# Down products of keys and values with the weights stationary, and latent rows split straight from PSUM

## The chip, the cores and the metric

One core of one Trainium2 chip. The metric is the device time of one execution in microseconds (us); each number given for the kernel is the median of several executions.

## What is computed

Eight sequences of 256 tokens (2048 rows of width 512) run through four blocks, each added to its input: a block-sparse linear layer, a routed bias (softmax over 64 experts, the best 8), an attention with latent keys and values, and a gated feed-forward. What the change touches is the beginning of the attention:

```python
kc = (hidden_states @ Wk_down.T).reshape(b, s, HK, L).transpose(0, 2, 1, 3)
vc = (hidden_states @ Wv_down.T).reshape(b, s, HK, L).transpose(0, 2, 1, 3)
lat = jnp.concatenate([kc, vc], axis=-1).reshape(b, s, HK * 2 * L)
k_cmp, v_cmp = jnp.split(lat, 2, axis=-1)
k = (k_cmp @ Wk_up.T).reshape(b, s, HK, D).transpose(0, 2, 1, 3)
v = (v_cmp @ Wv_up.T).reshape(b, s, HK, D).transpose(0, 2, 1, 3)
```

with HK = 8 heads, L = 32, D = 128, s = 256. The reshape in the third line mixes tokens and features: row 32 h + m of `lat` holds, for head h, the eight tokens 8 m to 8 m + 7 with their 32 key and 32 value latents each. So feature 64 j + (0 to 63) of a latent row comes from token 8 m + j.

## The kernel before, in words

All products on the matrix engine are made in three passes of fp32r operands, a high part and the rest (`PASSES`): high by high, low by high, high by low. ACT makes a high part (`hi_part`, a copy into fp32r), DVE or POOL the low part (`lo_part`, source less high part).

`first_stages` writes out one program for each engine. The work goes by steps s = 0 to 27 (`head_steps`). In step s the sparse linear layer (`SparseLinear`, 16 tiles of 128 tokens) works on tiles near s, and the routed bias (`RoutedBias`, 7 stages deep) on tiles near i = s - 5; its last stage turns the normed tile into `h3`, columns of tokens, high and low part. Step 18 is i = 13; the last product of the linear layer is in step 18. In each step PE, ACT and DVE first do the bodies of these two, then the key and value tasks assigned to the step; once the steps are over the other tasks follow without them. The order of the tasks is that of `kv_tasks`, the same on every engine, and each engine waits for its semaphores in this order. Tasks are made for each quad (half of the tokens, 1024 rows), and every task has a PSUM bank: `n % 4` in the steps, where banks 4 to 7 belong to the routed bias (and banks 0 to 3 to the linear layer up to step 19), then all eight in turn.

- A **Z** task (line 1280) makes the down product of 128 tokens, those at distance 8 from each other, times all 512 columns of key and value weights: 4 chunks of K by 3 passes, 12 matmuls of 512 columns. The tokens are the stationary operand, read from `h3` at a step of 8 elements (32 bytes). ACT copies the bank to `z`, which lies in the room of `w_raw` (line 1198).
- A **C** task (line 1284) turns 4 blocks of 128x128 of `z` with the unit matrix; the result holds latent features on partitions and latent rows along the columns. ACT and DVE make the two parts of `latent` from it (lines 69 and 74).
- A **K** task (line 1290) and a **V** task (line 1299) make the up products, 6 matmuls of 512 columns each. ACT copies the bank to a stage tile (line 1213), SP stores it to HBM.

There are 8 Z, 8 C, 16 K and 16 V tasks for each quad. In the steps, `head_steps` places 18 tasks of quad 0, from step 20 on (i = 15, once all 8 tiles of the quad are in `h3`). The weights for these products are loaded in 24 pieces (`kv_raw`), each split into parts by ACT and POOL: pieces 0 to 15 in steps 4 to 19, pieces 16 to 23 after step 27, each behind a K task on ACT.

DVE and ACT also make the token operands T1 to T4 of a later product (`TokenOperands`), 16 steps hung on tasks by the lists `sums`, `step_lo_at` and `step_stored`: DVE sums 2 or 3 times 128x512 (lines 358 to 369), ACT the high part, DVE the low part; the next sum waits for the low part before it. Steps 0 to 7 are stored to HBM by SP, three in their place between V stores and five after the last V store of quad 0, behind the store of three blocks of `h3`. Steps 8 to 15 belong to the K and V tasks of quad 1.

The attention then starts with line 1852 (`ps_q`).

## Time and profile before

| | us |
|---|---|
| median of 3 runs (lowest, highest) | 1645.33 (1645.15, 1645.78) |
| the profiled execution, its own time | 1645.85 |
| its span, first to last instruction | 1644.0 |
| PE busy (matmul) | 1615.2, 98% |
| DVE busy | 1163.2, 71% |
| ACT busy | 936.2, 57% |
| POOL busy | 830.8, 51% |
| last V matmul of the first stages ends, attention starts | 259.05 |

The span lacks 1.85 us of the execution's time, at its two ends. Busy times of PE are of overlapping instructions whose ends are modelled, so 98% doesn't say that PE runs at its peak; how far apart the starts of matmuls lie does. "PEld" is the load of a stationary operand, which runs beside the matmul before it.

### The profile page before, as it was taken

The numbers are of one execution on the slowest core, as the hardware profiler recorded it, in microseconds if no ns is written. First come the engines' busy times: TensorE is split into PE (matmuls) and PEld (weight loads), VectorE is DVE, ScalarE is ACT, GpSimd is POOL, SyncE is SP. The second block draws the span as 40 slices with busy tenths as digits, with TensorE's granted clock in tenths as the row PEclk, the third lists the DMA queues.
The fourth block names the chain that finished last, engine by engine and source line by source line (L and its number), as shares of the span: only waits on it lengthen the run. The fifth ranks groups of instructions, "written<-read, shape, count | busy, mean of one in ns | idle before, by whom it ended". The sixth has DMA issues, their size and how long they took to land.

```text
span 1644.0 us, 26456 instructions
## 1 busy us (share of the span) xinstructions
PE 1615.2 (98%) x8298; PEld 1368.8 (83%) x8298; DVE 1163.2 (71%) x2988; ACT 936.2 (57%) x2480; POOL 830.8 (51%) x1243
## 2 busy tenths in 40 slices
PE   7999999999999999999999999999999999999999
PEld 5778887888888888888888888888888788878887
DVE  7963365776776776777677767767767688787676
ACT  5865455665665765765666566657657443434432
POOL 6852004544634634644545445446446397709752
PEclk9999999999999999999999999999999999999999
DMA  5002753111111111134111111111111121102211
GB/s 187 24 18 83 282 197 123 39 65 39 52 65 39 52 64 39 44 100 183 47 52 39 65 40 52 65 39 52 65 40 26 41 70 64 39 32 91 64 65 52
DMA packets 62490, 114.99 MB, mean 70 GB/s; under 512 B 5584, under 2 KB 25040, under 8 KB 58256
## 3 DMA queue, kind: packets, MB, share of 16 engines
q1 hardware_dynamic: 62352, 113.30, 20.8%
q8 instruction: 68, 1.11, 0.3%
q14 instruction: 70, 0.57, 0.1%
HBM read 84.97 MB, written 28.31 MB: 69 GB/s over the span
## 4 chain that ended last, share of the span: by engine, by line
PE 90%; DVE 5%; issue 2%; ACT 1%; POOL 1%; DMA 1%; DVEq 0%; SPq 0%; POOLq 0%; ACTq 0%
PE ps_q L1912 21%; PE ps_q L1852 19%; PE f_ps_r L2393 11%; PE ps_o L1894 8%; PE f_ps_y L2412 7%; PE ps_s L1870 5%; PE ps_s L1882 5%; PE ps_s L1868 3%; PE kv_banks L1280 3%; PE kv_banks L1290 3%; PE kv_banks L1299 3%; PE f_ps_r L2377 1%; DVE bn_ln L97 1%; DVE h_lo L74 1%; DVE x L744 0%
## 5 line engine op out<-in xcount | busy, mean ns | idle before, releaser
L1912 PE MATMUL ps_q<-kv_w_hi,o_hi 128*128 128x512 f32 x512 | 202.2, 395 | 0.0
L1912 PE MATMUL ps_q<-kv_w_lo,o_hi 128*128 128x512 f32 x512 | 199.7, 390 | 0.0
L1912 PE MATMUL ps_q<-kv_w_hi,o_lo 128*128 128x512 f32 x512 | 199.6, 390 | 0.0
L74 POOL TENSOR_TENSOR kv_w_lo<-w_raw,kv_w_hi 128x512 fp32r<-128x512 f32 x128 | 163.2, 1294 | 56.3 <-ACT kv_w_hi L69 56.2
L1852 PE MATMUL ps_q<-h_hi,kv_w_hi 128*128 128x512 f32 x448 | 180.1, 402 | 0.1
L1852 PE MATMUL ps_q<-h_lo,kv_w_hi 128*128 128x512 f32 x448 | 175.1, 391 | 0.0
L1852 PE MATMUL ps_q<-h_hi,kv_w_lo 128*128 128x512 f32 x448 | 175.0, 391 | 0.0
L1681 DVE TENSOR_TENSOR x<-ps_q,x 128x512 f32<-128x512 f32 x128 | 88.1, 688 | 96.4 <-PE ps_q L1912 96.4
L69 ACT ACTIVATE kv_w_hi<-w_raw 128x512 fp32r<-128x512 f32 (+1 forms) x240 | 126.7, 567 | 45.5 <-POOL w_raw L300 42.0
L1495 ACT ACTIVATE prob<-prob,neg_max 128x128 f32<-128x128 f32 x256 | 100.4, 392 | 89.3 <-DVE neg_max L1651 89.3
L1440 POOL TENSOR_SCALAR prob<-prob,inv_sum 128x128 f32<-128x128 f32 x256 | 95.4, 373 | 109.5 <-DVE inv_sum L1656 109.4
L69 ACT ACTIVATE o_hi<-ps_o 128x512 fp32r<-128x512 f32 x128 | 76.3, 596 | 126.3 <-PE ps_o L1894 126.2
L74 POOL TENSOR_TENSOR h_lo<-v_raw,h_hi 128x512 fp32r<-128x512 f32 x32 | 41.3, 1291 | 184.8 <-ACT h_hi L69 184.8
L74 DVE TENSOR_TENSOR o_lo<-ps_o,o_hi 128x512 fp32r<-128x512 f32 x128 | 88.3, 690 | 56.2 <-ACT o_hi L69 56.1
L1497 ACT ACTIVATE prob<-prob,neg_max 128x256 f32<-128x256 f32 x256 | 127.0, 496 | 0.0
L1441 POOL TENSOR_SCALAR prob<-prob,inv_sum 128x256 f32<-128x256 f32 x256 | 122.8, 480 | 0.0
L1912 PEld LDWEIGHTS ps_q<-kv_w_lo,o_hi 128*128 128x128 f32 x512 | 96.1, 188 | 20.3
L1912 PEld LDWEIGHTS ps_q<-kv_w_hi,o_lo 128*128 128x128 f32 x512 | 96.3, 188 | 18.6
L1912 PEld LDWEIGHTS ps_q<-kv_w_hi,o_hi 128*128 128x128 f32 x512 | 96.2, 188 | 18.6
L295 POOL TENSOR_TENSOR w_raw<-w_raw 128x512 f32<-128x512 f32 x16 | 20.7, 1297 | 178.9 <-DVE kv_w_lo L74 178.9
L2393 PE MATMUL f_ps_r<-h_hi,kv_w_hi 128*128 128x512 f32 x280 | 109.1, 390 | 0.5 <-issue 0.4
L1882 PEld LDWEIGHTS ps_s<-ident,prob 128*128 128x128 f32 x768 | 91.2, 140 | 21.6 <-DVE prob_t_lo L74 3.9
(236 smaller groups left out, 4844.3 us busy)
## 6 DMA issues: line engine op xcount, KB each, us to landing
w_raw<-in_wq_g SPq DMA_DIRECT2D x16, 1024.0 KB, 4.8
w_raw<-in_wo_g SPq DMA_DIRECT2D x16, 1024.0 KB, 4.7
k_raw<-k_scratch SPq DMA_DIRECT2D x32, 256.0 KB, 3.4
v_raw<-v_scratch SPq DMA_DIRECT2D x32, 256.0 KB, 3.8
f_gate_raw<-in_gate_c SPq DMA_DIRECT2D x10, 512.0 KB, 4.9
f_up_raw<-in_up_c SPq DMA_DIRECT2D x10, 512.0 KB, 3.6
f_down_raw<-in_down_c SPq DMA_DIRECT2D x10, 512.0 KB, 4.1
x<-in_x SPq DMA_DIRECT2D x16, 256.0 KB, 2.8
```

Source lines behind the costliest of these rows:

```text
L69: return act.activation(parts[HI], src, ACT.Copy)
L74: return dve.tensor_tensor(parts[LO], src, parts[HI].bitcast(F32), ALU.subtract)
L1440: pool.tensor_scalar(prob[:, b, h, 0:P], prob[:, b, h, 0:P], inv_sum[:, b, h, 0:1], 1.0, ALU.mult, ALU.mult)
L1441: pool.tensor_scalar(prob[:, b, h, P:3 * P], prob[:, b, h, P:3 * P], inv_sum[:, b, h, 1:2], 1.0, ALU.mult, ALU.mult).then_inc(normed, 1)
L1495: act.activation(prob[:, b, h, 0:P], prob[:, b, h, 0:P], ACT.Exp, scale=-1.0, bias=neg_max[:, b, h, 0:1], accum_out=row_sum[:, b, h, 0:1])
L1497: act.activation(prob[:, b, h, P:3 * P], prob[:, b, h, P:3 * P], ACT.Exp, scale=-1.0, bias=neg_max[:, b, h, 1:2], accum_out=row_sum[:, b, ...
L1852: done = pe.matmul(ps_q[:, i, :], left[s][:, c, i * HEAD:(i + 1) * HEAD], right[t][:, c, :], start=(c == 0 and m == 0), stop=(c == 1 and m ...
L1882: done = pe.transpose(ps_t[:, (b + blk) % 2, h * P:(h + 1) * P], prob[:, b, h, blk * P:(blk + 1) * P], ident[:, :])
L1894: done = pe.matmul(ps_o[:, half, :], v[i][:, 2 * b + tile, :], prob_t[j][blk], start=(n == 0 and m == 0), stop=(n == len(blocks) - 1 and m ...
L1912: done = pe.matmul(ps_q[:, half, :], o[b][i][:, half, h, :], wo[j][:, h, :], start=(h == 0 and m == 0), stop=(h == GROUP - 1 and m == 2))
L2393: last = pe.matmul(bank(kind, k, name), stationary[a], feed.operand(right)[b][:, c, :], start=(c == 0 and m == 0), stop=(c == 1 and m == 2))
L2412: last = pe.matmul(ps_y[:, t % 4, :], inner[m, n][a][:, t % 4 * P:(t % 4 + 1) * P], down[m][b], start=(m == 0 and i == 0), stop=(m == chun ...
```

## The change

The Z task now takes 128 columns of the weights as its stationary operand and 512 tokens in a row (a pair of sequences) as the moving one. Its result has 128 down features (two heads, each with 32 key and 32 value latents, since the weights are packed by head) on partitions and tokens along the columns. That is already the orientation of `latent`, so z and the C tasks go away: ACT and DVE take the bank in four pieces each, one for each head of the two (`one`, a half of the source's partitions) and for odd and even tokens (`odd`, the half of the partitions that it goes to). A piece is 64 partitions by 4x2x32 = 256 elements, read from PSUM at a step of 8 elements. There are 4 Z tasks for each pair of sequences, 8 for each quad, still 12 matmuls of 512 columns each.

Tasks start in step 18 (i = 13), two in every step, 20 in all: 8 Z, 8 K of pair 0, 4 K of pair 1. All 24 pieces of weights are split in steps 4 to 27. Operand steps are hung on other tasks, and five instead of three are stored in their place between the V stores.

```diff
 def kv_tasks():
     for quad in range(2):
-        down = [("Z", quad, j, 0) for j in range(8)]
-        flip = [("C", quad, jp, hg) for jp in range(4) for hg in range(2)]
...
-        tasks += down[0:4] + flip[0:2] + down[4:6] + flip[2:4] + down[6:8] + flip[4:6]
-        tasks += (keys[0:2] + flip[6:8] if quad else flip[6:8] + keys[0:2]) + keys[2:] + values
+        tasks += [("Z", quad, pair, heads) for pair in range(2) for heads in range(KV_HEADS // 2)]
+        tasks += [("K", quad, pair, g) for pair in range(2) for g in range(KV_HEADS)]
+        tasks += [("V", quad, tile, part) for tile in range(8) for part in range(2)]
 def head_steps():
-    ready = TILES // 2 + RoutedBias.DEPTH
-    group = (2, 2, 3, 2, 2, 2, 3) + (2,) * (RoutedBias.STEPS - ready - 7)
+    ready = TILES + 2 - FIRST_ROUTED
...
-        count = group[i - ready] if i >= ready else 0
+        count = 2 if i >= ready else 0
 def first_stages(...):
             if not before:
                 if bank_of[n] >= 4:
                     eng.wait_ge(routed.lo_done, TILES)
+                elif bank_of[n] >= 2:
+                    eng.wait_ge(linear.x_done, TILES)
                 else:
                     eng.wait_ge(linear.lo_done, TILES)
-                    eng.wait_ge(linear.x_done, TILES)
...
+        def outlets(n):
+            _, _, pair, heads = tasks[n]
+            for one in range(2):
+                src = bank[one * HALF:(one + 1) * HALF, bank_of[n], :].rearrange("p (b m c o) -> p c b m o", b=2, c=4, o=2)
+                for odd in range(2):
+                    yield ([p[odd * HALF:(odd + 1) * HALF, :, 2 * pair:2 * pair + 2, 2 * heads + one, :] for p in latent], src[:, :, :, :, odd])
...
-        sums = [("V", 0, 0, 0), ("V", 0, 2, 0), ("V", 0, 4, 0), ("V", 0, 6, 0), ("Z", 1, 1, 0), ("Z", 1, 3, 0), ("Z", 1, 5, 0), ("Z", 1, 7, 0),
+        sums = [("V", 0, 0, 0), ("V", 0, 1, 1), ("V", 0, 2, 1), ("V", 0, 4, 0), ("V", 0, 5, 1), ("V", 0, 6, 1), ("Z", 1, 0, 2), ("Z", 1, 1, 2),
                 ("K", 1, 0, 4), ("K", 1, 0, 6), ("K", 1, 1, 0), ("K", 1, 1, 2), ("K", 1, 1, 4), ("K", 1, 1, 6), ("V", 1, 0, 0), ("V", 1, 2, 0)]
-        step_lo_at.update({at["C", 1, 2, 1]: 7, at["V", 1, 4, 0]: 15})
-        step_stored = {at[task]: j for j, task in enumerate((("V", 0, 2, 1), ("V", 0, 4, 1), ("V", 0, 6, 1)))}
+        step_lo_at.update({at["K", 1, 0, 1]: 7, at["V", 1, 4, 0]: 15})
+        step_stored = {at[task]: j for j, task in enumerate((("V", 0, 2, 0), ("V", 0, 3, 0), ("V", 0, 4, 1), ("V", 0, 6, 0), ("V", 0, 7, 0)))}
 # act_program, task(n)
                 if kind == "Z":
-                    act.activation(z[:, a // 2 % 2, :, a % 2, :].rearrange("p h (t l) -> p h t l", t=2),
-                                   bank[:, bank_of[n], :].rearrange("p (t h l) -> p h t l", t=2, h=KV_HEADS), ACT.Copy).then_inc(z_done, 1)
+                    for parts, src in outlets(n):
+                        hi_part(act, parts, src).then_inc(hi_done, 1)
 # dve_program, task(n)
-                if n in lo_count:
-                    dve.wait_ge(hi_done, lo_count[n])
-                    parts, src = outlet(n)
-                    lo_part(dve, parts, src).then_inc(lo_done, 1)
+                if n in parts_done:
+                    dve.wait_ge(linear.xb_done, TILES)
+                    for m, (parts, src) in enumerate(outlets(n)):
+                        dve.wait_ge(hi_done, parts_done[n] + m // 2 * 2 + 2)
+                        lo_part(dve, parts, src).then_inc(lo_done, 1)
 # pe_program, task(n)
                 if kind == "Z":
-                    pe.wait_ge(routed.lo_done, (quad + 1) * TILES // 2)
+                    pe.wait_ge(routed.lo_done, 4 * (2 * quad + a) + 4)
                     for c in range(KC):
                         for m, (u, v) in enumerate(PASSES):
-                            tokens = h3[u][:, c, quad * SPAN:(quad + 1) * SPAN].rearrange("p (n j) -> p n j", j=8)[:, :, a]
-                            last = pe.matmul(out, tokens, down_w[v][:, c, :], start=(c == 0 and m == 0), stop=(c == KC - 1 and m == 2))
-                elif kind == "C":
-                    pe.wait_ge(z_done, down_count[at[("Z", quad, 2 * a + 1, 0)]])
-                    for h in range(4):
-                        last = pe.transpose(out[:, h * P:(h + 1) * P], z[:, a % 2, 4 * b + h, :, :].rearrange("p j l -> p (j l)"), ident[:, :])
+                            last = pe.matmul(out, down_w[u][:, c, b * P:(b + 1) * P], h3[v][:, c, (2 * quad + a) * PAIR:(2 * quad + a + 1) * PAIR],
+                                             start=(c == 0 and m == 0), stop=(c == KC - 1 and m == 2))
                 elif kind == "K":
-                    if (a, b) == (0, 0):
-                        pe.wait_ge(lo_done, lo_count[at[("C", quad, 1, 1)]])
+                    if b == 0:
+                        latent_made(pe, quad, a)
```

The program of PE, steps 18 to 20, before: behind the last matmul of the linear layer (787) come three bodies of the routed bias (988 to 1018), and then the first matmul of a Z task (1280).

```order
255 L787 MATMUL kv_banks<-w_lo,h_hi 128x512
256 L988 MATMUL kv_banks<-ident,r_chosen 128x128
257 L996 MATMUL kv_banks<-ident,h 128x128 x4
...
260 L1018 MATMUL kv_banks<-ident,h 128x128 x4
261 L988 MATMUL kv_banks<-ident,r_chosen 128x128
...
265 L1018 MATMUL kv_banks<-ident,h 128x128 x4
266 L988 MATMUL kv_banks<-ident,r_chosen 128x128
...
270 L1018 MATMUL kv_banks<-ident,h 128x128 x4
271 L1280 MATMUL kv_banks<-kv_w_hi,h_hi 128x512
```

The same place of PE after the change (Z is line 1266 there).

```order
255 L786 MATMUL kv_banks<-w_lo,h_hi 128x512
256 L987 MATMUL kv_banks<-ident,r_chosen 128x128
257 L995 MATMUL kv_banks<-ident,h 128x128 x4
...
260 L1017 MATMUL kv_banks<-ident,h 128x128 x4
261 L1266 MATMUL kv_banks<-h_hi,kv_w_hi 128x512
...
284 L1266 MATMUL kv_banks<-h_lo,kv_w_hi 128x512
285 L987 MATMUL kv_banks<-ident,r_chosen 128x128
...
289 L1017 MATMUL kv_banks<-ident,h 128x128 x4
290 L1266 MATMUL kv_banks<-h_hi,kv_w_hi 128x512
```

Two Z tasks (24 matmuls) now stand behind the body of step 18 and of step 19 each, where bodies followed each other with nothing between them.

The program of ACT after the change, from the end of step 18 to the first half of step 19 (line 68 is `hi_part`).

```order
119 L933 ACTIVATE h1t<-kv_banks 128x512
120 L68 ACTIVATE kv_w_hi<-kv_raw 128x256
121 L68 ACTIVATE latent_hi<-kv_banks 64x4x2x32 x8
122 L903 ACTIVATE r_exp,r_total<-logits,r_neg_max 128x64
123 L908 ACTIVATE x<-x,r_combined 128x512
```

Before, the body of step 19 (904) followed at once on `kv_w_hi`; the eight pieces of 64 partitions now stand between them, and they wait for the Z tasks of their step.

## Rows read from the trace of the kernel before

**Rows 1.** The page: the span, the granted clock by 40th parts, and part 4, the chain by engine.

```profile
span 1644.0 us, 26456 instructions
...
PEclk9999999999999999999999999999999999999999
...
PE 90%; DVE 5%; issue 2%; ACT 1%; POOL 1%; DMA 1%; DVEq 0%; SPq 0%; POOLq 0%; ACTq 0%
```

**Rows 2.** The chain that ended last, in order of time: start us, us, what.

```profile
106.13 6.03 PE kv_banks L1280 x24
...
138.01 2.95 PE kv_banks L1280 x12
...
144.75 21.78 PE kv_banks L1290 x96
...
188.29 11.73 PE kv_banks L1280 x48
200.03 0.87 PE kv_banks L1284 x8
...
237.29 21.76 PE kv_banks L1299 x96
259.05 13.88 PE ps_q L1852 x60
...
274.99 6.19 DMA w_raw<-in_wo_g
```

**Rows 3.** Groups by form, 0 to 330 us: busy us, mean ns | idle us before them.

```profile
L1280 PEld LDWEIGHTS kv_banks<-kv_w_hi,h_lo 128*128 128x128 f32 x64 | 21.2, 331 | 0.2
...
L1290 PEld LDWEIGHTS kv_banks<-latent_hi,kv_w_lo 128*128 128x128 f32 x64 | 12.0, 188 | 2.4
...
L74 DVE TENSOR_TENSOR latent_lo<-kv_banks,latent_hi 128x512 fp32r<-128x512 f32 x16 | 10.3, 682 | 15.0 <-ACT latent_hi L69 15.0
...
L69 ACT ACTIVATE latent_hi<-kv_banks 128x512 fp32r<-128x512 f32 x16 | 8.8, 600 | 0.0
...
L914 ACT ACTIVATE r_chosen_t<-kv_banks 128x128 f32<-128x128 f32 x16 | 4.1, 258 | 0.2 <-PE kv_banks L988 0.2
...
L962 DVE TENSOR_TENSOR logits<-kv_banks,r_bias 128x64 f32<-128x64 f32 x16 | 3.4, 212 | 0.7 <-PE kv_banks L1010 0.7
```

**Rows 4.** Timeline of PE: start us, us, what [idle before <-releaser].

```profile
96.03 0.61 PE L1018 MATMUL kv_banks<-ident,h 128*128 128x128 f32 x4
97.97 0.30 PE L988 MATMUL kv_banks<-ident,r_chosen 128*128 128x128 f32 x1 [1.33 <-ACT h1t L934]
...
105.88 0.61 PE L1280 MATMUL kv_banks<-kv_w_hi,h_hi 128*128 128x512 f32 x1
...
112.00 0.27 PE L988 MATMUL kv_banks<-ident,r_chosen 128*128 128x128 f32 x1
...
114.60 0.61 PE L1280 MATMUL kv_banks<-kv_w_hi,h_hi 128*128 128x512 f32 x1
...
144.12 0.63 PE L996 MATMUL kv_banks<-ident,h 128*128 128x128 f32 x4 [0.99 <-DVE h_lo L74]
```

**Rows 5.** Timeline of ACT, the first and last instruction of step 18.

```profile
93.88 0.35 ACT L904 ACTIVATE r_exp<-logits,r_neg_max 128x64 f32<-128x64 f32 x1 [1.34 <-DVE r_neg_max L974]
...
97.72 0.41 ACT L69 ACTIVATE kv_w_hi<-kv_raw 128x256 fp32r<-128x256 f32 x1
```

**Rows 6.** Timeline of DVE, the first and last instruction of step 19.

```profile
98.59 0.66 DVE L744 TENSOR_TENSOR x<-kv_banks,x 128x512 f32<-128x512 f32 x1
...
103.25 0.17 DVE L101 BATCH_NORM_AGGREGATE mv_ln<-bn_ln 128x2 f32<-128x6 f32 x1
```

**Rows 7.** Timeline of ACT, the high parts of operand steps 8, 14 and 15.

```profile
223.42 0.62 ACT L69 ACTIVATE h_hi<-op_sum 128x512 fp32r<-128x512 f32 x1
...
241.94 0.63 ACT L69 ACTIVATE h_hi<-op_sum 128x512 fp32r<-128x512 f32 x1 [1.24 <-DVE op_sum L364]
...
251.47 0.63 ACT L69 ACTIVATE h_hi<-e_bias 128x512 fp32r<-128x512 f32 x1 [5.91 <-DVE e_bias L358]
```

More of the change, by code:

```diff
@@ L1026, in kv_tasks @@
     for quad in range(2):
-        down = [("Z", quad, j, 0) for j in range(8)]
-        flip = [("C", quad, jp, hg) for jp in range(4) for hg in range(2)]
-        keys = [("K", quad, pair, g) for pair in range(2) for g in range(KV_HEADS)]
-        values = [("V", quad, tile, part) for tile in range(8) for part in range(2)]
-        tasks += down[0:4] + flip[0:2] + down[4:6] + flip[2:4] + down[6:8] + flip[4:6]
-        tasks += (keys[0:2] + flip[6:8] if quad else flip[6:8] + keys[0:2]) + keys[2:] + values
+        tasks += [("Z", quad, pair, heads) for pair in range(2) for heads in range(KV_HEADS // 2)]
+        tasks += [("K", quad, pair, g) for pair in range(2) for g in range(KV_HEADS)]
+        tasks += [("V", quad, tile, part) for tile in range(8) for part in range(2)]
     return tasks
 def head_steps():
-    ready = TILES // 2 + RoutedBias.DEPTH
-    group = (2, 2, 3, 2, 2, 2, 3) + (2,) * (RoutedBias.STEPS - ready - 7)
+    ready = TILES + 2 - FIRST_ROUTED
     steps, n = [], 0
@@ L1056, in first_stages @@
     at = {task: n for n, task in enumerate(tasks)}
-    hi_order = [n for n, task in enumerate(tasks) if task[0] == "C"]
-    lo_count = {n: k + 1 for k, n in enumerate(hi_order)}
     down_order = [n for n, task in enumerate(tasks) if task[0] == "Z"]
-    down_count = {n: k + 1 for k, n in enumerate(down_order)}
+    parts_done = {n: 4 * k for k, n in enumerate(down_order)}
     stage_order = [n for n, task in enumerate(tasks) if task[0] in "KV"]
@@ L1068, in first_stages @@
         pieces_of = {"Z": KV_DOWN // KV_PIECE, "K": (KV_DOWN + KV_UP) // KV_PIECE, "V": KV_PIECES}
-        z = query.raw[:, :, :].rearrange("p (j h) (h2 t l) -> p j (h h2) t l", j=2, h2=4, t=2)
         bank = ps("kv_banks", [P, 8, HID], st)
@@ L1150, in pool_program, with store @@
                 routed.pool_body(pool, i)
-                if 0 <= p < HEAD_PIECES:
+                if 0 <= p < KV_PIECES:
                     piece_lo_part(pool, p)
-            for p in range(HEAD_PIECES, KV_PIECES):
-                piece_lo_part(pool, p)
             query.make(pool, 0)
+        def store(sp, n):
+            kind, quad, a, b = tasks[n]
+            if kind == "Z":
+                return
+            k = stage_count[n]
+            sp.wait_ge(staged, k + 1)
+            if k >= STAGES:
+                sp.wait_ge(stored[k % STAGES], 16 * (k // STAGES))
+            if kind == "K":
+                pair = 2 * quad + a
+                dst = k_scr[b, :, pair * PAIR:(pair + 1) * PAIR]
+            else:
+                pair = 2 * quad + a // 4
+                dst = v_scr[pair, :, a % 4, b * HID:(b + 1) * HID]
+            sp.dma_start(dst, stage_tile(k)).then_inc(stored[k % STAGES], 16)
+            if n in step_stored:
+                operands.store_step(sp, step_stored[n])
+            if n == at[("V", 0, 7, 1)]:
+                sp.wait_ge(routed.lo_done, TILES)
+                operands.store_blocks(sp)
+                for j in range(len(step_stored), 8):
+                    operands.store_step(sp, j)
+            if n == at[("K", 1, 0, 3)]:
+                query.load(sp, wq_g, 0)
@@ L1187, in act_program @@
+            for _, _, p, now in steps:
+                if 0 <= p < KV_PIECES - 2:
+                    load_piece(sp, p + 2)
+                for n in now:
+                    store(sp, n)
+            for n in range(paired, len(tasks)):
+                store(sp, n)
         def act_program(act):
@@ L1191, in task @@
                 if kind == "Z":
[L1192 to L1213 removed]
+                    for parts, src in outlets(n):
+                        hi_part(act, parts, src).then_inc(hi_done, 1)
+                else:
+                    k = stage_count[n]
+                    if k >= STAGES:
+                        act.wait_ge(stored[k % STAGES], 16 * (k // STAGES))
+                    if STAGED <= k < STAGED + STAGES:
+                        act.wait_ge(routed.lo_done, TILES)
+                    act.activation(stage_tile(k), bank[:, bank_of[n], :], ACT.Copy).then_inc(staged, 1)
                     if n in given_at:
@@ L1227, in act_program @@
                 routed.act_body(act, i)
-                if 0 <= p < HEAD_PIECES:
+                if 0 <= p < KV_PIECES:
                     piece_hi_part(act, p)
@@ L1293, in task @@
                 else:
-                    if (a, b) == (0, 0):
-                        pe.wait_ge(lo_done, lo_count[at[("C", quad, 3, 1)]])
+                    if a % 4 == 0 and b == 0:
+                        latent_made(pe, quad, a // 4)
                     for c in range(2):
```

68 lines of the change are left out of this document (9 added, 59 removed).

## The prediction, made before the change was run

> **What bounds the kernel now.** I read the page first. PE makes 90% of the chain that ended last, and its clock is the full one in all 40 slices, so the level of 2.4 GHz is not in question here; the span of 1644.0 us is PE's program plus its waits [rows 1]. Then I read that chain in order of time, which shows the places touched: Z tasks among the steps from 106.13 us, K tasks from 144.75, Z and C tasks of quad 1 from 188.29, the last V tasks until the attention starts at 259.05 [rows 2]. From 106 us on the chain lies on PE nearly all the time, so every microsecond that PE saves or idles there less is one off the whole. Third, the groups by form, for what a Z matmul waits for and what copies on ACT and DVE cost [rows 3]. Fourth, the timeline of PE: between 96 and 106 us, steps 18 to 20, PE waits for ACT and DVE behind each body, because no task is there yet [rows 4]; and those of ACT and DVE, for how full their steps are [rows 5, 6].
>
> **The change part by part.**
>
> *1. Turns go.* 64 turns leave PE. Eight take 0.87 us on the chain [rows 2], so 8 x 0.87 = **7.0 us**.
>
> *2. Z matmuls at another pace.* In quad 1, 48 matmuls take 11.73 us, 0.244 each; in quad 0, 24 take 6.03 and twelve 2.95, that is 0.251 and 0.246; I take 0.247 for the mean of all 192. K and V matmuls with the same 512 columns take 21.78 / 96 = 0.227 [rows 2]. The row of loads says why: a stationary operand read from tokens at a step of 8 elements takes 331 ns with 0.2 us of idle time in 64, one in a row takes 188 ns and leaves room [rows 3]. The new Z task loads weights in a row and moves tokens in a row, as K does, so I give it K's pace: 192 x 0.020 = **3.9 us**. I take this to be sure within 0.3.
>
> *3. Idle time before the first task.* The last four turns of step 18's body start at 96.03 [rows 4] and take half of the 0.87 us of eight [rows 2], so it ends at 96.47, and Z starts at 105.88. Between them lie two bodies, each 2.60 us when nothing is waited for (112.00 to 114.60) [rows 4]. 9.41 - 5.20 = **4.2 us** of idle, into which tasks now move: two Z behind the body of step 18 and two behind step 19's. PE does the same work, earlier.
>
> *4. The last wait of the steps.* Before, PE waited 0.99 us at 144.12, because short C tasks stood in the last steps [rows 4]; now two K tasks (2.7 us) stand in each of them. **1.0 us**.
>
> Together 16.1 us less. Against it:
>
> *5. Pieces on ACT and DVE.* A bank was copied to z and then split from a second bank; now it is split once, in four pieces of 256 elements on 64 partitions. No row shows such a piece. From 128 to 512 columns an ACT copy from PSUM goes from 258 to 600 ns [rows 3], so 256 lie at 258 + 342 / 3 = 0.37 us; on DVE 64 columns take 212 ns and 512 take 682 [rows 3], 1.05 ns for each more, so 256 lie at 0.41 us, of which 0.14 is fixed. That is my value, whole durations without overlap, since a piece changes its partitions from one to the next. The bound below is the same with the overlap seen between two instructions in a row, about 0.1 us less. The bound above: the only row that reads fp32 at a step of 8 elements is the weight load, 331 against 188 ns, a factor of 1.76; then a DVE piece is 0.14 + 0.27 x 1.76 = 0.62, and at the very most as long as 512 in a row, 0.68 [rows 3].
>
> Is that hidden? In the four steps with Z tasks (18 to 21) PE needs 2.6 + 24 x 0.227 + 0.1 for starting behind turns = 8.15 us. ACT needs its body, 93.88 to 98.13, 4.25 us [rows 5], and 8 x 0.37 = 3.0: 7.2 us. DVE needs 98.59 to 103.42, 4.83 us, with the linear layer's last sum in it [rows 6], and 8 x 0.41 = 3.3: 8.1 us. All three fit, DVE barely, and only in steps 18 and 19, since the linear layer's part is missing in 20 and 21. The covers are there because PE waits in each body for what the others did one step earlier. One wait is in the way: in step 19 the third Z task uses bank 2, free after the linear layer's last sum (DVE 744), which stands behind the pieces of step 18. Those end about 2.4 us after the second Z; then the sum, 0.7; PE comes after a body of 2.6. I take **0.4 us**.
>
> *6. Shorter steps 22 to 27.* Two K tasks are 2.7 us, a body 0.4 to 2.3, so a step is 3.2 to 5 us, while in each the low part of a tile must be ready for PE's next turn: a stage copy (0.5), ACT's body up to the high part (about 2.6 of the 4.25 [rows 5]), the split (0.6 and 0.7) come to about 4.3 us, where PE needs 4.1 in step 23. **0.3 us**. The pieces of weights now taken in these steps (0.41 us on ACT [rows 5], the rest on POOL) fit.
>
> *7. Quad 1.* ACT needs 4 x 0.37 = 1.5 and DVE 1.6 us for each Z of 2.72 us: fit. K waits for pieces of its own pair of sequences, with four Z or eight K tasks in between: 10.9 us ahead. SP issues the stores of operand steps 5 to 7 in front of the first K store, as it did with 3 to 7; but the low part of step 7 now comes behind the last Z, and the K stores, and so the stage tiles of ACT, wait for it: I reckon that ACT makes the high part of step 8 1.2 to 2.5 us later against the V tasks. From there the operand steps are paced by themselves: from step 8 at 223.42 to step 14 at 241.94, 3.1 us for each against 2.7 for two tasks of PE [rows 7], so the delay stays until step 15. At step 15 ACT stands until 251.47 [rows 7]; its next copy ends at 252.6, and PE, with 8 banks, would need it at 237.29 + 13 x 1.36 = 254.97 [rows 2]. Of these 2.4 us little or nothing is left. **0.3 us**.
>
> SP's own queue: piece loads now lie between K stores in other steps, two steps ahead of their use; the wait for the query weights moves by one K task, and they are needed 11 tasks later. No cost. POOL gets nothing but the last pieces of weights earlier. What follows 259.05 starts from the same work in the same order, so it moves as a whole.
>
> **Sum:** 7.0 + 3.9 + 4.2 + 1.0 - 0.4 - 0.3 - 0.3 = 15.1. The profiled execution took 1645.85 us (span 1644.0 and 1.85 around it); 1645.85 - 15.1 = 1630.75, and the median of the runs, 1645.33, lies 0.52 below the profiled one: **1630.2 us**.
>
> **The rivals.**
>
> *A. Pieces read slowly.* If a piece costs what the bound above says, DVE needs 4.8 + 8 x 0.62 = 9.8 us in a step where PE needs 8.15, ACT about 8.5. That is 1.6 us lost in each of up to four steps, less where the linear part is missing: 2 to 6 us, so 1632 to 1636. For it: 32 bytes between elements did slow the one row that has them. Against: that row is PE reading SBUF, this is ACT and DVE reading PSUM. The Trainium skill, SBUF — State Buffer, section "Door 1: The DMA port swizzle", speaks for it: PSUM has lines of 8 bytes, and each access that crosses to a new line pays; in a piece every element does. No row here shows it for ACT or DVE, and the page has no price; by the rule the time would be this rival's, about 1634.
>
> *B. Operand steps stop PE in quad 1.* If the delay in 7 is 4 us instead of 2, PE stands at V tasks 13 to 15 for about 2 us, and the attention's first weight parts are late by as much: 1632 to 1634. For it: a margin of 2.4 us; against: eight banks and that ACT catches up afterwards.
>
> *C. Nothing comes of it.* The time saved before 259 us is waited away later, at a wait that hangs on transfers and not on PE. For it: a transfer of 6.19 us lies in the chain at 274.99 [rows 2]; against: it fetches weights into a room that PE's own products and their sums must first give free, so it moves with them. 1643 to 1648.
>
> *D. Slower.* The pieces are the bound. Over the 64 pieces on DVE the loss is 32 d - 13.6 in the four steps (4 x (8 d + 4.8 - 8.2)) and 32 d - 27 in quad 1 (32 pieces and 5.6 us of operand steps against 21.8 us of Z and 10.9 of K tasks). It eats 15.1 us at d = 0.87 us, over twice my value; at d = 1.2 us the loss is 36, and the time 1645.3 - 15.1 + 36 = 1666. Nothing in the profile has 256 elements that slow.
>
> That the change doesn't do what it says can hardly be: tokens as moving operand and weights as stationary ones in a row stand in the program.
>
> **How the numbers follow.** My forecast (1628 to 1632) 0.62; A 0.16; B 0.12; C 0.05; D 0.03; 0.02 for less than 1628. With the costs of 5 to 7 at nothing the time is 1645.33 - 16.1 = 1629.2, and the gains may be mis-sized by 1 us, so the range starts at 1628.0; it reaches to 1635.5, most of A and all of B. 0.2% of the time is 3.3 us, about what can be told from no change. Faster by more than that: 0.92; within it, C in the main: 0.05; slower: 0.03.
>
> **What would show it.** Right if: Z matmuls are 0.227 us apart and their loads 190 ns; no turns of z; PE starts Z at about 96.4 and idles under 1 us in the steps; the attention starts at 243 to 245 us; pieces of 0.35 to 0.45 us. Wrong if: DVE or ACT pieces show 0.6 us or more and PE's idle time ahead of 987 or 995 is released by them (A); PE waits at V tasks of quad 1 for copies (B); the start of the attention moves by 15 us and the end by less (C).

## The result, and the profile after

The changed kernel takes **1637.45 us** (median of 5 runs, 1636.5 to 1638.69) against 1645.78 us (5 runs, 1645.15 to 1646.75) of the kernel before in the same session; the ratio is 0.9945, with a 95% interval of 0.9934 to 0.9957. The gain is 8.3 us where 15.1 were forecast, and the time lies 1.95 us above the end of the range (1635.5). The profiled execution took 1638.69 us with a span of 1636.8: 7.2 us less than the profiled one of before, and this is the sum that the rows below have to explain. It was the slowest of the five; its mean granted clock is 0.998, that of the next three 0.999, that of the fastest 1.000.

The page of the changed kernel, as in [rows 1]: 64 matmuls fewer, and a clock that the slices of 41 us still show as full.

```profile
span 1636.8 us, 26389 instructions
...
PE 1607.9 (98%) x8234; PEld 1352.8 (83%) x8234; DVE 1179.7 (72%) x3036; ACT 942.5 (58%) x2512; POOL 830.4 (51%) x1243
...
PEclk9999999999999999999999999999999999999999
```

The chain that ended last, in order of time (start and duration in us, engine, what), as in [rows 2]. L1266 is now Z, L1273 K, L1282 V, L1835 the first products of the attention.

```profile
96.93 5.50 PE kv_banks L1266 x24
106.28 5.49 PE kv_banks L1266 x24
...
152.58 8.18 PE kv_banks L1273 x36
160.76 21.76 PE kv_banks L1282 x96
182.52 21.76 PE kv_banks L1266 x96
204.28 21.76 PE kv_banks L1273 x96
226.04 10.89 PE kv_banks L1282 x48
246.62 5.97 PE kv_banks L1282 x18
252.59 13.87 PE ps_q L1835 x60
```

The 96 Z matmuls of quad 1 take 21.76 us, 0.227 each, as K and V do; before there were 96 matmuls, the first 48 of them 0.244 us apart and the others 0.250, and 32 turns between them. Z starts at 96.69 (the chain counts it from 96.93), forecast 96.4. But the pairs of Z tasks in the steps follow one another at 9.35 us instead of 8.15 (96.93, 106.28, and two more), and quad 0 ends at 182.52, only 5.8 us earlier than the 188.29 of [rows 2]. And of quad 1's V phase, which without a stop is 21.76 us, 26.55 are gone when the attention starts at 252.59: 6.5 us earlier than 259.05. The rest of the program takes 1384.2 us after it, before 1385.0; so 5.8 + 0.7 + 0.7 = 7.2.

By groups of one form (line, engine, operation, busy us, mean ns of one, idle time before), as in [rows 3], from 96 to 226 us: the load of weights in a row, and the pieces.

```profile
L1266 PEld LDWEIGHTS kv_banks<-h_hi,kv_w_lo 128*128 128x128 f32 x64 | 12.0, 188 | 2.4
```

ACT's groups of the changed kernel:

```profile
L68 ACT ACTIVATE latent_hi<-kv_banks 64x256 fp32r<-64x256 f32 x64 | 24.2, 378 | 10.5 <-PE kv_banks L1266 9.2
```

DVE's groups of the changed kernel:

```profile
L73 DVE TENSOR_TENSOR latent_lo<-kv_banks,latent_hi 64x256 fp32r<-64x256 f32 x64 | 27.0, 423 | 17.4 <-ACT latent_hi L68 15.7
```

A piece takes 0.378 us on ACT and 0.423 on DVE, where 0.37 and 0.41 were taken. So the length of the pieces is not what was mis-sized. Where does PE stand, then? First the steps, in PE's timeline (start, duration, operation, and in brackets the idle time before it with who ended it), as in [rows 4]:

```profile
102.25 0.27 PE L987 MATMUL kv_banks<-ident,r_chosen 128*128 128x128 f32 x1
...
103.66 1.00 PE L1009 MATMUL kv_banks<-router,h1t 128*128 128x64 f32 x8
105.65 0.63 PE L1017 MATMUL kv_banks<-ident,h 128*128 128x128 f32 x4 [0.99 <-ACT r_chosen_t L913]
...
136.37 0.63 PE L995 MATMUL kv_banks<-ident,h 128*128 128x128 f32 x4 [0.75 <-DVE h_lo L73]
```

PE waits 0.99 us ahead of the last turns of the body of step 19, and so it does in steps 20 and 21, for `r_chosen_t`, a copy of ACT. Each wait costs 1.2 us of pace (9.35 less 8.15). ACT and DVE at this time, where [rows 5, 6] showed steps without tasks:

```profile
99.72 1.58 ACT L68 ACTIVATE latent_hi<-kv_banks 64x256 fp32r<-64x256 f32 x4 [1.29 <-PE kv_banks L1266]
102.45 1.58 ACT L68 ACTIVATE latent_hi<-kv_banks 64x256 fp32r<-64x256 f32 x4 [1.14 <-PE kv_banks L1266]
104.06 0.35 ACT L903 ACTIVATE r_exp<-logits,r_neg_max 128x64 f32<-128x64 f32 x1
...
104.41 0.80 ACT L908 ACTIVATE x<-x,r_combined 128x512 f32<-128x512 f32 x1
105.23 0.28 ACT L913 ACTIVATE r_chosen_t<-kv_banks 128x128 f32<-128x128 f32 x1
```

DVE's timeline of the changed kernel:

```profile
103.33 1.78 DVE L73 TENSOR_TENSOR latent_lo<-kv_banks,latent_hi 64x256 fp32r<-64x256 f32 x4 [0.95 <-ACT latent_hi L68]
105.14 0.69 DVE L743 TENSOR_TENSOR x<-kv_banks,x 128x512 f32<-128x512 f32 x1
```

The four pieces of the second Z task start at 102.45, when its last matmul is done, and `r_chosen_t` of the *next* body stands behind them. PE's last turns (L1017) go to the bank that this copy empties. It empties it in the same step, not one step behind. In step 19 a second wait lies under this one: its first Z task needs bank 2, which DVE's sum of the linear layer (L743) frees at 105.83, while PE, at a pace of 8.15 us, would have come at 96.69 + 8.15 = 104.84. Steps 20 and 21 have no such sum.

Second, quad 1: DVE, then SP's queue, then ACT, then PE.

```profile
209.52 1.78 DVE L73 TENSOR_TENSOR latent_lo<-kv_banks,latent_hi 64x256 fp32r<-64x256 f32 x4 [1.57 <-ACT latent_hi L68]
211.34 0.69 DVE L73 TENSOR_TENSOR op_out_lo<-e_bias,op_out_hi 128x512 fp32r<-128x512 f32 x1
```

SP's timeline of the changed kernel:

```profile
212.06 0.32 SPq L387 DMA_DIRECT2D operand_scratch<-op_out_hi  x1
212.42 0.43 SPq L387 DMA_DIRECT2D operand_scratch<-op_out_lo  x1
212.95 1.90 SPq L1167 DMA_DIRECT2D k_scratch<-kv_stage  x4
```

SP's timeline of the kernel before, the first K stores of quad 1:

```profile
218.24 2.36 SPq L1173 DMA_DIRECT2D k_scratch<-kv_stage  x3
```

ACT's timeline of the changed kernel:

```profile
215.85 0.60 ACT L1201 ACTIVATE kv_stage<-kv_banks 128x512 f32<-128x512 f32 x1 [3.53 <-DMA k_scratch<-kv_stage]
216.35 0.62 ACT L68 ACTIVATE h_hi<-op_sum 128x512 fp32r<-128x512 f32 x1
...
235.94 0.63 ACT L68 ACTIVATE h_hi<-op_sum 128x512 fp32r<-128x512 f32 x1 [1.24 <-DVE op_sum L363]
...
245.45 0.63 ACT L68 ACTIVATE h_hi<-e_bias 128x512 fp32r<-128x512 f32 x1 [5.89 <-DVE e_bias L357]
```

PE's timeline of the changed kernel:

```profile
246.62 0.71 PE L1282 MATMUL kv_banks<-kv_w_hi,latent_hi 128*128 128x512 f32 x1 [2.90 <-ACT kv_stage L1201]
...
248.83 0.63 PE L1282 MATMUL kv_banks<-kv_w_lo,latent_hi 128*128 128x512 f32 x1
249.26 0.63 PE L1282 MATMUL kv_banks<-kv_w_hi,latent_hi 128*128 128x512 f32 x1
...
250.11 0.42 PE L1282 MATMUL kv_banks<-kv_w_lo,latent_hi 128*128 128x512 f32 x1
```

The low part of operand step 7 (211.34) comes behind the pieces of all Z tasks; SP issues the stores of step 7's high and low part at 212.06 and 212.42, and only then that of the first K tile, 13.1 us ahead of the first V task (226.04); before it was 19.1 us ahead (218.24 and 237.29). ACT had waited 3.53 us for that stage tile. It makes the high part of step 8 at 216.35, 9.7 us ahead of the first V task, where [rows 7] had 223.42, 13.9 us ahead. The shift of 4.2 us is still there at step 14 (235.94, 9.9 us behind the start of V; before 241.94, 4.7 us behind it: 5.2). At step 15 ACT stands until 245.45, all eight banks are full, and PE stops for 2.90 us. The wait of ACT itself is no part of the change: it is 5.89 us where the kernel before had 5.91. In both, DVE first makes two low parts of query weights, and two of the three sums of step 15 then take 1.66 us each, where those of the other steps take 0.69. Behind the stop the matmuls are 0.427 us apart until 250.1, and a window of the trace (us, then busy time of each engine, granted clock, DMA share and GB/s) gives the clock:

```profile
245.00:250.00 5.00, 3.38 (x8) 2.71 (x9) 1.71 (x3) 4.38 (x9) 1.63 (x1) 0.67 0.50 193
```

0.67 in the mean of these 5 us, in which PE first idled and then ran at 1.2 GHz; from 250.1 on it is 2.4. The eight matmuls at the low level take 3.49 us instead of 1.82, another 1.7 us. A second such stretch lies at 275 to 280 us (clock 0.75), with a wait of 1.64 us for DVE in it. Neither comes in every execution: the fastest of the five, at 1636.5 us, has a mean clock of 1.000. The Trainium skill, TensorE: Matmul & The Clock Gate, section "Back-to-back issue gap", gives N / 1.2 ns between isolated matmuls of N columns at the low level and N / 2.4 + 2.5 at the high one, which for 512 columns makes an estimate of 427 and 216 ns. The trace agrees with the first (0.427 us) and shows 0.227 us for the second.

So two places hold what is missing: about 3.6 us in the steps (call it loss 1) and 4.6 in quad 1 (2.9 + 1.7, loss 2). Both readings are of a trace, and each has a rival: loss 1 may come from pieces that are too long rather than from where they stand, loss 2 from the extra work of ACT and DVE rather than from the place of step 7.

### The profile page after: what moved, and what is told of

The parts are those of the page before. It is cut to its first block, busy times and chain, and to the rows that moved or that the text cites. A ratio compares the mean times of both kernels' runs of the same rounds, so it can differ in the third digit from the quotient of the medians.

```text
span 1636.8 us, 26389 instructions
## 1 busy us (share of the span) xinstructions
PE 1607.9 (98%) x8234; PEld 1352.8 (83%) x8234; DVE 1179.7 (72%) x3036; ACT 942.5 (58%) x2512; POOL 830.4 (51%) x1243
## 4 chain that ended last, share of the span: by engine, by line
PE 93%; DVE 2%; ACT 2%; POOL 1%; issue 1%; DMA 1%; SPq 0%; DVEq 0%; ACTq 0%; POOLq 0%
PE ps_q L1895 21%; PE ps_q L1835 19%; PE f_ps_r L2376 11%; PE ps_o L1877 8%; PE f_ps_y L2395 7%; PE ps_s L1853 5%; PE ps_s L1865 5%; PE ps_s L1851 3%; PE kv_banks L1266 3%; PE kv_banks L1273 3%; PE kv_banks L1282 2%; PE kv_banks L786 2%; PE f_ps_r L2360 1%; PE kv_banks L1002 1%; PE kv_banks L1009 0%
## 5 line engine op out<-in xcount | busy, mean ns | idle before, releaser
L1835 PE MATMUL ps_q<-h_hi,kv_w_hi 128*128 128x512 f32 x448 | 180.7, 403 | 0.1
L1835 PE MATMUL ps_q<-h_lo,kv_w_hi 128*128 128x512 f32 x448 | 175.5, 392 | 0.0
L1835 PE MATMUL ps_q<-h_hi,kv_w_lo 128*128 128x512 f32 x448 | 175.2, 391 | 0.0
L2376 PE MATMUL f_ps_r<-h_hi,kv_w_lo 128*128 128x512 f32 x280 | 108.9, 389 | 0.0
```

The lines of the kernel that those rows point to most:

```text
L1835: done = pe.matmul(ps_q[:, i, :], left[s][:, c, i * HEAD:(i + 1) * HEAD], right[t][:, c, :], start=(c == 0 and m == 0), stop=(c == 1 and m ...
L2376: last = pe.matmul(bank(kind, k, name), stationary[a], feed.operand(right)[b][:, c, :], start=(c == 0 and m == 0), stop=(c == 1 and m == 2))
```

## The experiments

All kernels are edits of the changed kernel; "span" and places in it are of their profiled execution. The ratio is to the kernel before, run on the same chip in the same session. Its median went from 1645.78 to 1647.27 us from session to session, so medians of two sessions compare to about 1.5 us; the places in the traces are the sharper measure.

### e_late: pieces and copies one step later

```diff
+            held = ()
             for s, i, p, now in steps:
...
-                for n in now:
+                for n in held:
                     task(n)
-            for n in range(paired, len(tasks)):
+                held = now
+            for n in list(held) + list(range(paired, len(tasks))):
                 task(n)
```

The same in ACT's and in DVE's program; PE's order stays.

> The changed kernel, but in steps 18 to 27 ACT and DVE do the tasks of a step only after the body of the next step. Theory 1 (my own now): in steps 19 to 21 PE's last turns wait, within the same step, for ACT's copy of the chosen weights (0.99 us each, three times, and 9.35 us from one step's first Z to the next instead of 8.15), because that copy stands behind eight pieces which wait for the Z tasks. Expected: these waits gone, 8.15 to 8.3 us for a step, the last V task of quad 0 ends 4 to 4.5 us earlier (182.5 to about 178), the whole 1633 to 1634 us. Theory 2: the pieces themselves are the load (ACT 7.4, DVE 8.4 us a step); then the order makes no difference and a step stays over 9 us. The V tasks of quad 1 keep their wait of 2.9 us by both.

Measured: 1634.55 us (1633.93 to 1635.1), ratio 0.9931 (0.9916 to 0.9946). The chain, and the groups of PE from 96 to 253 us that have idle time:

```profile
97.06 5.47 PE kv_banks L1270 x24
105.22 5.47 PE kv_banks L1270 x24
...
179.62 21.76 PE kv_banks L1270 x96
```

PE's groups of e_late:

```profile
L1286 PE MATMUL kv_banks<-kv_w_hi,latent_hi 128*128 128x512 f32 x64 | 25.6, 400 | 2.7 <-ACT kv_stage L1201 2.7
...
L995 PE MATMUL kv_banks<-ident,h 128*128 128x128 f32 x36 | 5.4, 274 | 1.3 <-DVE h_lo L73 1.3
```

The pairs are 8.16 us apart, what the prediction worked out for PE alone; the waits for `r_chosen_t` are gone, with pieces of the same length. In their place 1.3 us stand at L995 in step 23 (0.75 in the changed kernel). Quad 0 ends 2.9 us earlier, at 179.62, where about 178 was expected. Loss 1 is the order: the bodies of ACT and DVE stand behind the pieces. In steps 20 and 21 this is the copy alone; in step 19 the edit also puts the linear layer's sum ahead of the pieces, at 99.02, and the run doesn't part the two. The stop in the V phase stays at 2.7 us.

### e_flat and e_stay: are the pieces slow?

e_flat reads 256 neighbouring elements for each piece instead of elements at a step of 8, so that a latent row gets other tokens:

```diff
-yield ([p[odd * HALF:(odd + 1) * HALF, ...] for p in latent], src[:, :, :, :, odd])
+flat = bank[one * HALF:(one + 1) * HALF, bank_of[n], 256 * odd:256 * odd + 256].rearrange("p (c b m) -> p c b m", c=4, b=2)
+yield ([p[odd * HALF:(odd + 1) * HALF, ...] for p in latent], flat)
```

> The changed kernel, but each piece reads 256 neighbouring elements of its bank instead of every eighth and so on, so that the latents are of other tokens. If elements read at a step of 8 from PSUM are slow, ACT's 378 ns and DVE's 423 ns for a piece fall clearly (below 0.33 and 0.36), and steps 19 to 21 get shorter by over 1 us. If not (my theory), both stay within 10 ns, and the time within 0.5 us.

Measured, one execution: 1636.69 us, span 1634.9. The pieces:

```profile
L68 ACT ACTIVATE latent_hi<-kv_banks 64x256 fp32r<-64x256 f32 x64 | 24.2, 378 | 10.5 <-PE kv_banks L1267 9.2
```

DVE's groups of e_flat:

```profile
L73 DVE TENSOR_TENSOR latent_lo<-kv_banks,latent_hi 64x256 fp32r<-64x256 f32 x64 | 27.0, 423 | 17.4 <-ACT latent_hi L68 15.7
```

378 and 423 ns, the same to the nanosecond, and the pairs stay 9.34 us apart. Reading PSUM at a step of 32 bytes costs ACT and DVE nothing here. The Trainium skill, SBUF — State Buffer, section "Door 1: The DMA port swizzle", gives PSUM lines of 8 bytes and says that an access pattern which isn't contiguous slows matmuls; it gives no rule for ACT and DVE. Rival A had carried the rule over to them, and for these reads of fp32 the measurement doesn't bear that out.

e_stay sends each piece to the half of the partitions that it is read from, so that keys and values of the two heads are mixed up in `latent`:

```diff
-p[odd * HALF:(odd + 1) * HALF, :, 2 * pair:2 * pair + 2, 2 * heads + one, :]
+p[one * HALF:(one + 1) * HALF, :, 2 * pair:2 * pair + 2, 2 * heads + odd, :]
```

> The changed kernel, but each piece goes to the same half of the partitions that it comes from (odd tokens to the other head's place, so the latents are mixed up). In the changed kernel four pieces take 1.58 us on ACT and 1.78 on DVE, each starting when the one before is done (0.40 and 0.45 apart), while copies of 512 columns started 0.1 us before the end of the last. If the change of partitions from piece to piece forbids this overlap, pieces now come 0.30 (ACT) and 0.35 us (DVE) apart, and steps 19 to 21 get shorter by 0.3 us or so each. If it is not that, nothing changes.

Measured, one execution: 1634.46 us, span 1632.7. In the timelines of ACT and DVE:

```profile
99.39 1.32 ACT L68 ACTIVATE latent_hi<-kv_banks 64x256 fp32r<-64x256 f32 x4 [1.28 <-PE kv_banks L1266]
```

DVE's timeline of e_stay:

```profile
100.14 1.55 DVE L73 TENSOR_TENSOR latent_lo<-kv_banks,latent_hi 64x256 fp32r<-64x256 f32 x4 [1.50 <-ACT latent_hi L68]
```

PE's groups of e_stay from 94 to 253 us:

```profile
L1282 PE MATMUL kv_banks<-kv_w_hi,latent_hi 128*128 128x512 f32 x64 | 25.0, 391 | 1.4 <-ACT kv_stage L1201 1.4
```

Four pieces take 1.32 us instead of 1.58 on ACT and 1.55 instead of 1.78 on DVE, though one piece alone is as long as before (372 and 418 ns): where the output stays in the same partitions, an instruction starts while the one in front of it still runs (on ACT 0.32 us apart in the mean instead of 0.40, on DVE 0.38 instead of 0.45; the output changes its half once among the four). The prediction had taken the durations whole for this reason. The Trainium skill, VectorE: DVE Perf Modes, section "Two Vector instructions with no wait between them", holds an instruction whose output starts in another group of partitions than the last output; on DVE the trace agrees, and the price is 0.07 us in this mean. On DVE the SBUF input of a piece (`latent_hi`) changes its half together with the output, so this run doesn't part the two; on ACT only the output changes. That section doesn't speak of ACT.

The pairs come to 9.07 us apart and the waits for `r_chosen_t` to 2.2 us, so the length of the pieces has a part in loss 1, but a small one: 0.3 us a step, of 1.2. In loss 2 its part is larger. With step 7 at its old place, the high part of step 8 comes at 213.28, 11.2 us ahead of V (224.50) instead of 9.7, the stop falls from 2.9 to 1.4 us, and no matmul behind it is slow. The attention starts at 248.55, 4.0 us earlier than in the changed kernel.

### e_store7, e_early: what stops PE in quad 1?

e_store7 moves the two stores of step 7 in SP's queue behind the fourth K store:

```diff
-                for j in range(len(step_stored), 8):
+                for j in range(len(step_stored), 7):
                     operands.store_step(sp, j)
             if n == at[("K", 1, 0, 3)]:
+                operands.store_step(sp, 7)
```

> The changed kernel, but SP stores operand step 7 behind the fourth K store of quad 1 instead of ahead of the first. Theory 1: the high part of step 8 waits for a stage tile, whose store waits in SP's queue for the low part of step 7; then it comes 1.5 to 2 us earlier (6.7 to 6.3 us... that is at about 8 us before the V tasks of quad 1 start less, from 9.7 us to over 11 us ahead of them), PE's wait of 2.9 us at the fourteenth V task shrinks to 1 us or so, and the half clock behind it (3.8 us of granted 1.2 GHz) shrinks or goes: 1634.5 to 1636.5 us. Theory 2: the operand steps are late because of their own sums (DVE), not because of the store: nothing moves, 1637 to 1638.

Measured: 1635.49 us (1635.32 to 1636.06), ratio 0.9937 (0.9923 to 0.9952). The stop, and the clock around it:

```profile
L1283 PE MATMUL kv_banks<-kv_w_hi,latent_hi 128*128 128x512 f32 x64 | 25.0, 391 | 2.1 <-ACT kv_stage L1202 2.1
```

And the window of e_store7, with the clock behind the busy times:

```profile
245.00:250.00 5.00, 4.37 (x18) 3.30 (x18) 1.29 (x2) 4.82 (x10) 2.49 (x2) 1.00 0.78 299
```

The high part of step 8 comes at 213.65, 11.9 us ahead of V (225.52) instead of 9.7, but the stop falls only from 2.9 to 2.1 us: from step 8 to step 14 (234.59) it now takes 20.9 us, where the changed kernel took 19.6 and the kernel before 18.5. No matmul behind the stop is slow, but this can't be put down to the edit: in e_flat, with a stop of 2.83 us at the same place, none is slow either (0.23 us apart from 245.87 on). Half a confirmation: the first K tile comes sooner, and at step 8 what ends last is now DVE's sum, still behind the last pieces. Later ACT waits 3.67 us for a K store (until 221.28, ahead of step 10), where the changed kernel waited 2.09. I take this for the price of the two stores that now stand in front of the later K stores; no run shows it alone.

e_early takes up both at their root, the sums of steps 6 and 7:

```diff
-("V", 0, 6, 1), ("Z", 1, 0, 2), ("Z", 1, 1, 2),
+("V", 0, 6, 1), ("Z", 1, 0, 0), ("Z", 1, 0, 3),
...
-step_lo_at.update({at["K", 1, 0, 1]: 7, at["V", 1, 4, 0]: 15})
+step_lo_at.update({at["Z", 1, 1, 0]: 7, at["V", 1, 4, 0]: 15})
```

> The changed kernel, but operand steps 6 and 7 hang on the first and fourth Z task of quad 1 (not on the third and seventh), and the low part of step 7 on the fifth Z task (not on the second K task). Theory 1: PE's wait of 2.9 us in the V tasks of quad 1 comes from step 7's low part standing behind the pieces of all eight Z tasks; from it SP's queue, the K stores, and the high part of step 8 (9.7 us ahead of the V tasks, 13.9 before the change) are late, and all later steps. Now the high part of step 8 comes about 3 us earlier, over 12.5 us ahead of the V tasks; PE's wait in the V tasks goes, and with it the half clock behind it; 1632.5 to 1634 us. Theory 2: the operand steps are held by their transfers (ACT waited 2.4 to 3.0 us for stores in each of steps 2 to 5): then they come no earlier, and the time stays above 1636.

Measured: 1633.87 us (1633.64 to 1634.29), ratio 0.9922 (0.9907 to 0.9937). ACT's timeline, and what is left of PE's idle time there:

```profile
213.88 0.63 ACT L68 ACTIVATE h_hi<-op_sum 128x512 fp32r<-128x512 f32 x1 [0.86 <-DVE op_sum L357]
...
242.00 0.63 ACT L68 ACTIVATE h_hi<-e_bias 128x512 fp32r<-128x512 f32 x1 [5.91 <-DVE e_bias L357]
```

PE's groups of e_early:

```profile
L1835 PE MATMUL ps_q<-h_hi,kv_w_hi 128*128 128x512 f32 x7 | 2.8, 403 | 0.5 <-issue 0.5
```

The high part of step 8 is at 213.88, 12.0 us ahead of V (225.92), that of step 15 at 242.00; no V task waits, and no matmul of the phase is slow. The attention starts at 248.19, 4.4 us earlier than in the changed kernel, and the span is 4.7 us shorter, with the same work on every engine. So the place of steps 6 and 7 is enough to bring or remove loss 2. It is not the only thing that counts: e_stay, with shorter work at the old place, took away half of the stop. The delay of step 8 is made of both, what stands in front of it and how long that takes.

### e_start20: what was the early start worth?

`ready` two steps later, so Z starts in step 20 and 16 tasks lie in the steps:

```diff
-    ready = TILES + 2 - FIRST_ROUTED
+    ready = TILES + 4 - FIRST_ROUTED
```

> The changed kernel, but tasks start in step 20 as they did before, 16 of them in the steps. If the early start gives what I forecast less what the in-step waits take (4.2 against 2 x 1.2), the last V of quad 0 ends 1.5 to 2 us later than in the changed kernel, and the whole takes 1639 to 1640. If starting early is worth its full 4.2 us, it is 1641 to 1642; if it is worth nothing, 1637 to 1638.

Measured: 1640.77 us (1640.01 to 1641.4), ratio 0.9967 (0.9955 to 0.998): 3.3 us more than the changed kernel, between the two ranges that were expected. That is what the early start is worth here, its 4.2 us less what it brings, to about 1 us: by the ratios it is 3.6, and the attention starts 2.7 us later (255.33). Two bodies wait 1.3 us each for ACT's `h1t` (2.7 us at L987), one instead of three waits at L1017 (1.0 us), and behind the wait of 1.35 us at 102.38 the turns and products are slow (granted clock 0.76 from 100 to 106 us):

```profile
102.38 0.30 PE L987 MATMUL kv_banks<-ident,r_chosen 128*128 128x128 f32 x1 [1.35 <-ACT h1t L933]
...
103.77 1.92 PE L1002 MATMUL kv_banks<-e_bias,r_chosen_t 128*128 128x512 f32 x2
```

Two matmuls of 512 columns take 1.92 us where the changed kernel's take 1.02. In the kernel before they took 1.02 at the same place behind the same wait (1.34 us), so such a wait need not bring the slow turns.

### e_both, e_all, e_mix: both repairs together

e_both has the edits of e_late and e_early, e_all that of e_store7 as well.

> Both edits: tasks in the steps done by ACT and DVE after the next step's body, and operand steps 6 and 7 earlier. If the two losses are apart from each other, they add: 2.9 us (e_late against the changed kernel) and what e_early gives; 1629.5 to 1631.5 us, which is my forecast for the change itself.

> As the one with both edits, and step 7 stored behind the fourth K store as well. If the V tasks' wait is gone already, nothing more comes of it: within 0.5 us of the other. If some wait is left, up to 1 us less.

Measured: e_both **1631.05 us** (1630.4 to 1631.15), ratio 0.9904 (0.9887 to 0.992); e_all 1632.03 (1631.85 to 1632.66), ratio 0.9911 (0.9897 to 0.9926). The chain of e_both:

```profile
179.69 21.76 PE kv_banks L1270 x96
...
223.21 21.76 PE kv_banks L1286 x96
```

The V phase of quad 1 takes its 21.76 us, and the attention starts at 245.29, 1.3 us behind what the prediction's terms give (259.05 - 15.1 = 243.95). The waits left are 1.3 us at L995 and 0.3 ahead of the attention, where those terms hold 1.0 us of losses, and Z starts 0.5 us later than forecast (96.88); 0.2 us are not assigned. Together the repairs bring the start of the attention 7.3 us forward, alone 3.1 (249.53) and 4.4: they add up. In e_all the third repair costs 1.0 us, where at most 0.5 was expected: the stores of step 7 now stand in front of later K tiles, and a stop of 1.1 us is back in the V phase.

e_mix lags only the tasks of Z by a step and leaves K and V copies in their own:

```diff
-                for n in held:
+                for n in list(held) + [n for n in now if tasks[n][0] != "Z"]:
                     task(n)
-                held = now
+                held = [n for n in now if tasks[n][0] == "Z"]
```

> Lags only the splits of Z tasks by one step on ACT and DVE (copies of K and V tasks are done in their own step again), with the operand sums 6 and 7 at the earlier tasks. Theory: the wait of 1.3 us at the turns of h (995) in step 23 comes from the chain of a step, in which lagged copies stand; with copies of K tasks in their own step as in the changed kernel it falls to about 0.75 us (what the changed kernel showed there), the waits at 1017 stay away, and the attention starts 0.5 us earlier, at about 244.8; time 1630.5. Rival: in step 22 the lagged pieces and the step's own copies stand together on ACT, four tasks in one step, and the wait is as long or longer (1.3 to 2.5 us): 1631 to 1632.

Measured: 1630.69 us (1630.55 to 1630.76), ratio 0.9904 (0.9887 to 0.992). The wait at L995 is 1.28 us at 136.84, the same as in e_both, so the theory of this run fell: the wait doesn't depend on where the K copies of step 22 stand. The span is 0.5 us shorter, but its Z tasks start at 96.25 where e_both's start at 97.13, and the attention at 244.63 against 245.29: this difference of 0.9 us lies ahead of the first instruction that the edit moves, so these runs don't make one faster than the other. What sets the wait in step 23 stays open beyond its releaser, DVE's `h_lo`.

## Why the prediction was wrong

The sign held, and the gains were sized well. The time was wrong because two covers were taken as given which the trace of before could not show, and which the new order took away.

- **1, turns (7.0 us), and 2, pace of Z (3.9).** Right. Of quad 1, e_early shows 65.8 us from the end of quad 0 to the attention, the changed order of work without a stop; before it was 70.8. The difference of 5.0 is half of 10.9 less the 0.5 us at L1835.
- **3, idle time before the first task (4.2).** The early start was right: Z at 96.7 against 96.4, within the scatter of this place (96.0 in e_mix to 96.9 in e_both, ahead of anything that those edits move). e_start20 finds it worth 3.3 us net of the waits that it brings.
- **5, pieces.** Their size was nearly right: 0.378 and 0.423 us for 0.37 and 0.41, but on DVE they start 0.45 us apart, so eight take 3.6 us and not 3.3. With a body of 4.83 us this makes 8.4 us, over the 8.15 of PE, in the step with the linear layer's sum. That was not what cost the time: in e_late the same work goes at 8.16. The step that failed is the sentence "The covers are there because PE waits in each body for what the others did one step earlier." The copy `r_chosen_t` is awaited in the same step. ACT had to do the pieces of a Z task that had just ended (102.45), 1.2 us of its body, and then this copy, while PE had products only until 104.66. **0.4 us were forecast; 3 x 1.2 = 3.6 came.** The forecast 0.4 us were for bank 2 in step 19. That wait was mis-sized too: the bank came free 1.0 us behind PE's time, hidden under the wait for the copy. Adding up busy time tells whether the work fits, not whether it is in time. The program of ACT printed before the prediction already had the eight pieces in front of the whole body.
- **4 and 6.** The wait of 0.99 us at 144.12 is gone. At L995 the changed kernel waits 0.75 us, forecast 0.3.
- **7, quad 1.** The right mechanism with the wrong sizes. The step that failed is "I reckon that ACT makes the high part of step 8 1.2 to 2.5 us later against the V tasks": it was 4.2, and 5.2 at step 14, against the margin of 2.4 us, which was right (5.2 - 2.4 = 2.8, and PE stood 2.9). The prediction had the chain in full (low part behind the last Z, K stores behind it, stage tiles behind them) but shows no working for its size; the first K store came 6.0 us later against the V tasks, the high part 4.2. Nor did the delay stay as it was: steps 8 to 14 took 19.6 us instead of 18.5, with ACT waiting for K stores ahead of steps 9 and 10. And the price of the stop left out the clock: 1.7 us for eight matmuls at 1.2 GHz, in those executions that have them. **0.3 us were forecast; 4.6 came.**

The two excesses, 3.2 and 4.3, with 0.4 in 6 and 0.3 for the start, make 8.2 us; 0.7 us gained behind the start of the attention goes the other way. 15.1 - 8.2 + 0.7 = 7.6, against 7.2 in the profiled executions; 0.4 us is not assigned. That the medians differ by 8.3 fits the clocks: 3.5 us at 1.2 GHz lower the mean of 1637 us by 0.001, and the profiled execution, at 0.998, had both slow stretches where the median one had room for one.

Of the rivals, **B** (0.12) was the mechanism of quad 1, with 2.9 us of stop at the fourteenth V task for its "about 2 us", and it came on top of loss 1, which no rival had. **A** is refuted by e_flat: its symptom, PE's idle time in the bodies released by ACT and DVE, did appear, but the step of 8 elements had no part in it. **C** did not happen: from e_both to the changed kernel 7.3 us at the start of the attention are 7.4 us of the span. **D** was far off. The range ended at 1635.5 because each case was taken alone; with B's 2 to 4 us and 3 of a wait in the steps together it would have ended at 1637.2, still 0.25 us short of the time. With both places repaired the change comes to about what was forecast for it: 1631.05 and 1630.69 against 1630.2. There is some luck in this, since the waits left in e_both are not those of terms 5 and 7.

## What to carry to other kernels

When work is moved beside other work, don't stop at the sum of busy times for a step: take each wait of the engine that sets the pace, ask whether what it waits for is made in the same step or one earlier, and count what now stands in front of it on its engine. Follow a queue to its end: a low part that is late held up a store, that a stage tile, that a copy 34 us later (211.34 to 245.45). An engine's copies of what was just computed belong behind its part of the next body, if banks allow it, and a stop of PE of some 3 us should be priced with and without matmuls at half clock behind it: both came here.

## What the runs showed of the hardware

- ACT and DVE read fp32 from PSUM at a step of 32 bytes as fast as in a row (378 and 378 ns, 423 and 423, for 64x256), while PE's weight load from SBUF at that step takes 331 ns instead of 188 [rows 3].
- For these pieces, on both engines, instructions overlap more where the output (on DVE one input with it) stays in the same partitions: 0.32 against 0.40 us apart on ACT, 0.38 against 0.45 on DVE.
- After a stop of 2.9 us PE's matmuls were 0.427 us apart for 3.5 us. After 2.7 us in e_late they started at the full pace, were 0.427 apart from 244.63 to 247.61, and then at 0.23 again; after 2.83 us in e_flat and 2.1 us in e_store7 they stayed at 0.23. In the kernel before, two waits of 1.3 us in a row left the clock alone, in e_start20 one of them was followed by turns at half clock. What decides between these is open.
